# Rotary embedding in the QKV stage: two 256-wide multiplications against one packed table in place of eight 64-wide ones

## The reference

```python
xn = layernorm(x)                                  # x: (4, 2048, 2048), fp32
x  = x + attention(xn) + ffn(xn)
# attention: 16 query heads and 4 key/value groups of 128
Q = rope(xn @ Wq + bq);  K = rope(xn @ Wk + bk);  V = xn @ Wv + bv
# rope on one head of 128 columns, halves x1 and x2 of 64 columns, tables cos and sin (position x 64)
rope(x) = concat(x1 * cos - x2 * sin,  x1 * sin + x2 * cos)
# then scores with a sliding window of 512 and 4 sink keys, softmax, @ V, @ Wo + bo
# ffn: top-2 of 8 LoRA experts over a shared W1/W3/W2 FFN of 7168
```

## Time and profile before

| | us |
|---|---|
| median of 3 runs | 3154.51 |
| lowest, highest | 3150.71, 3155.93 |
| the profiled execution | 3149.4 |
| its span, slowest core (core 4) | 3147.9 |
| shortest span of the eight cores (core 5) | 3124.6 |

### The profile page before, as it was taken

How to read it: one execution, slowest core, us unless ns; L and a number is a source line. 1 busy time by engine, 2 the same in 40 slices (tenths; PEclk the granted TensorE clock), 3 DMA queues, 4 the chain that set the end, 5 groups by cost and what they waited for, 6 DMA issues and landing times. The chain is left out here.

```text
span 3147.9 us, 39246 instructions; the slowest of 8 cores (3124.6 to 3147.9 us)
## 1 busy us (share of the span) xinstructions
PE 2552.4 (81%) x13656; PEld 1290.3 (41%) x13656; DVE 1632.7 (52%) x3496; ACT 577.0 (18%) x934; POOL 205.2 (7%) x210
## 2 busy tenths in 40 slices
PE   1365676676694599999999999999999999999994
PEld 1244464444341244444444444444444444444442
DVE  7577756888402153545445453545445354545433
ACT  2100005777420020111102020110202011110200
POOL 0000000000000110010101010010101001010000
PEclk9999997777797799999999999999999999999996
DMA  4533210000352473534527263452617254452406
GB/s 135 108 41 41 28 15 21 1 1 1 41 67 41 48 80 44 47 52 39 66 25 84 33 65 51 41 64 27 78 16 88 41 50 56 36 65 27 54 1 213
DMA packets 305586, 160.02 MB, mean 51 GB/s; under 512 B 233706, under 2 KB 293490, under 8 KB 301554
## 3 DMA queue, kind: packets, MB, share of 16 engines
q0 software_dynamic: 299616, 123.25, 34.2%
q1 hardware_dynamic: 5778, 34.26, 3.3%
HBM read 272.35 MB, written 8.39 MB: 89 GB/s over the span
## 5 line engine op out<-in xcount | busy, mean ns | idle before, releaser
L1136 PE MATMUL pfa<-big 128*128 128x512 bf16 x2432 | 626.9, 383 | 26.0 <-DVE a2acc L1157 26.0
L1168 DVE TENSOR_TENSOR sumT<-pfa,sumT 128x512 bf16<-128x512 f32 x448 | 309.8, 692 | 521.3 <-PE pfa L1136 456.9
L1030 PE MATMUL pfa<-xnTo,w1b 128*128 128x512 bf16 x1792 | 406.7, 381 | 53.1 <-DMA w3b<-w3t 32.1
L1091 DVE TENSOR_TENSOR x1sb<-pfa,b1sb 128x512 f32<-128x512 f32 x224 | 153.7, 686 | 489.3 <-ACT b3sb L1060 482.7
L1033 PE MATMUL pfa<-xnTo,w3b 128*128 128x512 bf16 x1792 | 405.1, 379 | 0.0
L1136 PEld LDWEIGHTS pfa<-big 128*128 128x128 bf16 x2432 | 238.3, 98 | 320.2 <-issue 38.4
L1136 PE MATMUL pfa<-big,w2x 128*128 128x512 bf16 x1152 | 345.9, 382 | 16.8 <-DVE a2acc L1157 11.6
L1030 PEld LDWEIGHTS pfa<-xnTo,w1b 128*128 128x128 bf16 x1792 | 174.4, 98 | 269.4 <-issue 61.9
L1033 PEld LDWEIGHTS pfa<-xnTo,w3b 128*128 128x128 bf16 x1792 | 175.0, 98 | 211.7
L1066 ACT ACTIVATE s1sb<-x1sb 128x512 f32<-128x512 f32 x224 | 141.0, 630 | 556.7 <-DVE x3sb L1096 556.7
L417 PE MATMUL pq<-wr,xnTo 128*128 128x256 bf16 x1536 | 183.3, 275 | 21.9 <-DMA wr<-wq 21.9
(11 more groups left out here) (135 smaller groups left out, 2326.5 us busy)
## 6 DMA issues: line engine op xcount, KB each, us to landing
w1b<-w1t POOLq DMA_DIRECT2D x56, 512.0 KB, 9.2
w3b<-w3t POOLq DMA_DIRECT2D x56, 512.0 KB, 11.3
big<-w2t POOLq DMA_DIRECT2D x19, 1024.0 KB, 14.5
xin<-xkv SPq DMA_DIRECT2D x13, 1024.0 KB, 6.0
w2x<-w2t POOLq DMA_DIRECT2D x9, 1024.0 KB, 10.7
wr<-wq POOLq DMA_DIRECT2D x8, 1024.0 KB, 10.9
wow<-wo POOLq DMA_DIRECT2D x8, 1024.0 KB, 9.4
xr<-xkv SPq DMA_DIRECT2D x8, 1024.0 KB, 8.9
```

The lines of the kernel that those rows point to most:

```text
L1030: te.matmul(pfa[m % 2][:, :], w1b[sl][:, hh * 128:(hh + 1) * 128], xnTo_s(hh, tc), start=(hh == 0), stop=(hh == HT - 1))
L1091: v.tensor_tensor(x1sb[k][:, :], pfa[4 + k][:, :], b1sb[m % 2][:, :], ALU.add)
L1136: ins = te.matmul(pfa[gidx % 4][:, :], ap_[:, (j % 2) * D + h * 128:(j % 2) * D + (h + 1) * 128], x2v(k)[:, j * TOK + tc * 512:j * TOK + ( ...
L1168: _inc(v.tensor_tensor(dst, pfa[gidx % 4][:, :], dst, ALU.add), ve_b)
```

## The change

The host packs, for each token tile, cos and sin into one table row of 320 columns: cos, sin, cos, sin, cos. One multiplication of the 256 columns of qscr with columns 0 to 255 of this row gives q1*cos and q2*sin of both heads; a second with columns 64 to 319 gives q1*sin and q2*cos. Both go to rop, which is now laid out by kind of product and not by head. The four subtractions and additions keep their sizes and read rop at other places. The tables are loaded whole, by two transfers in place of four, and VectorE's wait at L427 counts five transfers in place of seven. In bytes a partition, the tables of Q go from 2 x 2048 to 10240, those of K from 2 x 3328 to 16640.

```diff
-    cqtd = nc.dram_tensor("cqt", [128, NTT * 64], F32, kind="ExternalInput")
-    sqtd = nc.dram_tensor("sqt", [128, NTT * 64], F32, kind="ExternalInput")
-    cktd = nc.dram_tensor("ckt", [128, NKT * 64], F32, kind="ExternalInput")
-    sktd = nc.dram_tensor("skt", [128, NKT * 64], F32, kind="ExternalInput")
+    cqtd = nc.dram_tensor("cqt", [128, NTT * 320], F32, kind="ExternalInput")
+    cktd = nc.dram_tensor("ckt", [128, NKT * 320], F32, kind="ExternalInput")
...
-                for dst, src in ((cqs, cqtd), (sqss, sqtd), (cks, cktd), (sks, sktd),
+                for dst, src in ((cqs, cqtd), (cks, cktd),
                                  (bqbs, bqbd), (bkbs, bkbd), (bvbs, bvbd)):
...
-                        _w(v, d_const, qd + 7 * 16)
+                        _w(v, d_const, qd + 5 * 16)
...
+                    tab = cqs if kind == "q" else cks
+                    base = sub * 320
                     _w(v, pe_b, qp2 + (i - 2) + 1)
                     qr = qrot[i % 2]
-                    for hd in range(2):
-                        o = hd * 128
-                        r = hd * 256
-                        q1 = qscr[:, o:o + 64]
-                        q2 = qscr[:, o + 64:o + 128]
-                        v.tensor_tensor(rop[:, r:r + 64], q1, ctab, ALU.mult)
-                        v.tensor_tensor(rop[:, r + 64:r + 128], q2, stab, ALU.mult)
-                        v.tensor_tensor(rop[:, r + 128:r + 192], q1, stab, ALU.mult)
-                        ins = v.tensor_tensor(rop[:, r + 192:r + 256], q2, ctab, ALU.mult)
+                    v.tensor_tensor(rop[:, 0:256], qscr[:, :],
+                                    tab[:, base:base + 256], ALU.mult)
+                    ins = v.tensor_tensor(rop[:, 256:512], qscr[:, :],
+                                          tab[:, base + 64:base + 320], ALU.mult)
                     rope_ves[i] = _inc(ins, ve_s)
                     _w(v, ve_s, rope_ves[i])
                     for hd in range(2):
                         o = hd * 128
-                        r = hd * 256
-                        v.tensor_sub(qr[:, o:o + 64], rop[:, r:r + 64], rop[:, r + 64:r + 128])
-                        ins = v.tensor_add(qr[:, o + 64:o + 128], rop[:, r + 128:r + 192],
-                                           rop[:, r + 192:r + 256])
+                        v.tensor_sub(qr[:, o:o + 64], rop[:, o:o + 64],
+                                     rop[:, o + 64:o + 128])
+                        ins = v.tensor_add(qr[:, o + 64:o + 128], rop[:, 256 + o:256 + o + 64],
+                                           rop[:, 256 + o + 64:256 + o + 128])
...
+def _pack_cs(c, s, n):
+    out = np.empty((128, n * 320), np.float32)
+    for t in range(n):
+        cc = c[:, t * 64:(t + 1) * 64]
+        ss = s[:, t * 64:(t + 1) * 64]
+        out[:, t * 320:(t + 1) * 320] = np.concatenate([cc, ss, cc, ss, cc], 1)
+    return out
```

More of the change, by code:

```diff
@@ L320, in build_program @@
               for i in range(3)]
[L321 to L324, removed]
+        cqs = qkv_ctx.enter_context(nc.sbuf_tensor("cqs", [128, NTT * 320], F32))
+        cks = qkv_ctx.enter_context(nc.sbuf_tensor("cks", [128, NKT * 320], F32))
         bqbs = qkv_ctx.enter_context(nc.sbuf_tensor("bqbs", [128, D], BF16))
@@ L1258, in _rope_tables @@
     sk = sk.reshape(NKT, 128, 64).transpose(1, 0, 2).reshape(128, NKT * 64)
-    return (np.ascontiguousarray(cq), np.ascontiguousarray(sq),
-            np.ascontiguousarray(ck), np.ascontiguousarray(sk))
+    return (np.ascontiguousarray(_pack_cs(cq, sq, NTT)),
+            np.ascontiguousarray(_pack_cs(ck, sk, NKT)))
 def _mask_for(h):
@@ L1292 @@
     for h in range(2):
-        cq, sq, ck, sk = _rope_tables(h)
-        per_h[h] = dict(cqt=cq, sqt=sq, ckt=ck, skt=sk, maskb=_mask_for(h))
+        cq3, ck3 = _rope_tables(h)
+        per_h[h] = dict(cqt=cq3, ckt=ck3, maskb=_mask_for(h))
     in_maps = []
```

## The result

The changed kernel takes 3121.4 us in the median of 8 runs, and its ratio to the kernel before is 0.990, 95% interval 0.9887 to 0.9913: of 3154.5 us, 31.5 us less (27 to 36). The forecast was 3124.5 us, 29.9 us less. Ten executions of the kernel before, those shown ahead and seven more, have a median of 3192.1 us, 70.8 above the changed kernel's, because five of them were disturbed; the ratio leaves disturbed runs of both kernels out.

What follows compares the result with a forecast made beforehand. VectorE's 3.38 us loop per item, closed through TensorE's transposes, was taken to bound the Q and K part. Multiplications at -37.1 us and table bytes at +7.2 sum to -29.9, from 3154.5 to 3124.5 us; range 3115 to 3141.

Steps and rivals of the forecast that it cites:

- The bound: Q and K part of qkv: VectorE's loop, closed through TensorE's transposes and the copy, sets 3.38 us an item.
- Eight into two: Multiplications in Q and K: two of 256 columns save 0.417 us an item, 37.1 us over 89 loops.
- PE's wait for qrot: Sign in the Q and K loop: TensorE's wait for qrot, 1.24 us before, would be near 0.8 us.
- The tables' bytes: Start of qkv: 2.06 MB more of tables delay the first matmul by 7.2 us, bounds 3.8 to 14.7.
- the overlap of the queues: Start of qkv: queues take turns packet by packet, so 720 weight packets between SP's 720 add 3.15 us.
- the rate: Start of qkv: SP's 4.23 MB move at the earlier 0.279 MB/us and need 15.2 us.
- The base: Whole kernel: start from the 3154.5 us median of the runs shown, with their spread of 3150.7 to 3155.9.
- Later stages: Scores, output projection, routing and FFN issue loads after stage gates, so they shift as a whole; V is unchanged.
- A: Rival on Q and K multiplications: durations count in full, 75 us saved, 3079.5 us; chance 0.05.
- B: Rival at the start of qkv: tables land so late that all 90 items start late, 3169.5 us; chance 0.04.
- C: Rival in Q and K: TensorE's clock falls to 1.2 GHz, 58 us slower, 3212 us; chance 0.01.
- D: Rival after qkv: something later has its own date and the gain vanishes there, 3154.5 us; chance 0.05.

Runs made afterwards that it cites:

- deferred copy: Changed kernel with VectorE's copy of item i-1 put behind the additions of item i: ratio 0.9718 to the kernel before, loop 2.20 us.
- four-way cut: Changed kernel with each 256-wide multiplication cut in two of 128 columns: ratio 0.9952 to the kernel before, loop 3.11 us.
- wide tables alone: Changed kernel with the eight 64-wide multiplications put back, reading the packed row: ratio 1.0019 to the kernel before.
- K table late: Changed kernel with the K table and the biases of K and V asked for only after eight items: ratio 0.9868 to the kernel before.
- narrow tables: Two 256-wide multiplications with the four small tables of the kernel before, 64 columns read four times with a step of zero: ratio 0.9883 to that kernel.
- combined kernel: Four small tables read with a step of zero, two multiplications, two wide additions, copy behind the next item's additions: ratio 0.9625 to the kernel before.

## What held, and the step that failed

**The bound.** That VectorE, the transposes and the copy close the loop, though neither engine is full, was read from one item's timeline. The deferred copy shows it: 0.77 us an item came out with no instruction removed.

**Eight into two.** 0.417 us an item was forecast, and the loop went from 3.38 to 2.97 us. Over 90 items the cores show 36.7 us against 37.1. The start distance of 256 columns, interpolated as 0.335 us, is 0.34, and the duration 0.42. The four-way cut put 128 columns on the same line, at 0.20 us. PE's wait for qrot was forecast near 0.8 us and is 0.94: it fell by 0.41, but from the 1.35 us of most items and not from the 1.24 of the one that was read.

**The tables' bytes, the step that failed.** +7.2 us was forecast, +6.0 measured, and +5.8 with the wide tables alone. The bytes are on the path and the size lies within its bounds (3.8 to 14.7), but the term was mis-sized and its working is wrong in two places.

The first is the overlap of the queues. The equal totals of the earlier trace rows, 1008 and 984, were read as turns from start to end, so that all 720 packets of SP would have a weight packet between them. The turns are real, and hold for long rows too (331 and 333 on the core shown, and equal to 3% on all eight), but only while both queues have packets; before, they are equal to 3% on five cores, and on the other three the weights have 1.2 to 1.4 packets for one of SP's. Before that SP's queue runs alone, because the weights' first packet starts 3.6 to 5.8 us after its request, in both kernels; behind SP's last packet the weights run alone. That the totals came out equal was chance: at SP's last packet the weights of that core had 720, those of the others 803 to 1321.

The second is the rate. With the engines full in this stretch, before and after, what delays the first product is the engine time of SP's added bytes, nearly whatever the order; no run changed the order alone. Added up over the packets up to the first product and averaged over the eight cores, SP's packets take 7.6 us of 16 engines before and 13.4 after, 5.8 us more, for a start 6.0 us later. With the K table late they take 5.8 us, 1.9 less than before, for a start 1.9 us sooner; with the narrow tables 7.6, for 0.2 later. The forecast had 15.2 us for 4.23 MB, at the 0.279 MB/us of shorter rows, and these took 13.4, or 0.31 MB/us. That alone would make the term 7.5 in place of 5.8; the packet count took 0.3 off again.

**The base.** The forecast set out from 3154.5 us, the median of three executions, and took their spread (3150.7 to 3155.9) for its range. It has no term for an execution outside that spread. With the plain medians, 3192.1 and 3121.4, the difference is 70.8 us, more than twice the 29.9 that was forecast; by the ratio the change is worth 31.5. (3154.5 less 29.9 is 3124.6; the prediction has 3124.5.)

**Later stages.** They shifted as a whole: 2654.3 us before and 2652.5 after from the last V product to the end, and 2649 to 2660 in all the experiments.

**The rivals.** A (durations in full, -75 us) falls by the result and by the four-way cut. B (tables last) falls by the first VectorE wait, which ends on TensorE, and by SP's packets, all through by 133 us and so ahead of the first product. C (the clock) falls with the granted clock of 1.00 at 69% busy, and at 98% in the combined kernel. D (given back) falls by the table of stages.

## What to carry to other kernels

Price short instructions on an in-order engine by the distance between their starts, and only the last one before a wait by its duration; interpolate both from widths that the trace has. A loop can be closed through two engines with neither full: find it in the timeline of one item, and look first for a wait to be covered by the next item's work, which here was worth 71 us, where the fewer multiplications gave 37. Equal totals of two queues in a window do not show that they take turns: cut the window where both run, and price added bytes by their engine time. Before tables are copied out to make operands contiguous, try a step of zero, and count what each byte delays if it is loaded beside the first thing that the stage waits for.

## What was not expected of the hardware

While SP's hardware queue and the software queue of casting weight loads both had packets, the engines took them one for one on most cores, whatever the rows' length: 334 to 332 with rows of 1 to 4 KB, 331 to 333 with rows up to 16 KB, though a weight packet is 0.5 KB. So the weights got 17.6% of the engines' time beside long rows, where they got 39.2% beside short ones. The first weight packet started 3.6 to 5.8 us after its request, and till then SP's queue had the engines alone. A table operand of 64 fp32 columns repeated four times with a step of zero ran as fast as 256 contiguous ones, 0.42 us. TensorE kept the granted clock of 1.00 while busy for 98% of 174 us.
